# A transformer block in software pipeline on one core: outputs and feed-forward of a ahead of b, swaps and rotation in the turn of their projections

## The chip, the cores and the metric

The kernel runs on one core of a Trainium2 chip. Times are device microseconds of that core. A core has TensorE (PE in the profile, its weight loads as PEld), VectorE (DVE), ScalarE (ACT), GpSimd (POOL) and SyncE (SP), each with its own instruction queue that it works through in order; they wait for one another on semaphores. Here SP issues all DMAs.

## The reference, cut to what matters

Sixteen sequences of 512 tokens by 256 go through four residual steps, all in f32:

```python
x = x + attn_a(layernorm(x))   # 16 heads of 16, biases; window of |i-j| <= 32 and 4 global rows and columns; softmax
x = x + ffn(layernorm(x))      # int weights / 127; h = silu(gate) * up, 768 wide
x = x + attn_b(layernorm(x))   # num = exp(rotated q . k / 4), causal; den = sum(exp(unrotated q . k / 4)) over ALL keys
x = x + ffn(layernorm(x))      # the same weights
```

Attention b forms two sets of scores: of plain queries and keys for the denominator (512 keys, no mask), and of rotated ones for the numerator (causal).

## The kernel before, in words

**Slots.** Work is cut by sequence and pipelined in *slots*. In slot k each *block* of work handles sequence k minus its lag (`LAG`, a negative lag is a sequence ahead). The blocks: PA, VA, A are projections to queries and keys, values, and attention of a; OA its output projection and residual; F1 the first feed-forward; PB, VB, B, OB the same for attention b; RB the rotation; F2 the second feed-forward; NA the first layer norm of the next sequence. There are 20 slots, -1 to 18; slots 3 to 14 are a hardware loop of 12 turns, the others are written out. `ORDER` is the order in which the dense blocks take the two shared PSUM banks `gu_bank`; their counts (`GU`) turn it into semaphore values.

**The order of the work** is a table. `AT` gives each step a place on a line of about 125 units per slot; `places()` sorts them into `PLACES`, and every engine's function `slot()` walks that list and emits its part. So the same table sets the order on all five queues. The table's numbers are places, not times.

**Steps that the change touches.** Names are kinds in `PLACES`, lines those of the profile.
- *Projection* (T, PE L1038): six matmuls into a `gu_bank`; T1 on ACT takes the high half (L1174 of a, L1181 of b), T2 on DVE the low half (L1442, L1446); for b DVE also multiplies by cos into `tmp` (L1449).
- *Swap* (W, PE L1046): two matmuls with a permutation bring odd and even dimensions across. W1 on DVE multiplies by sin into `turned`, which lies in x1 (L1457). W2 is POOL's addition to `tmp` (L1563), ACT's high half (L1189), POOL's low half (L1565). The third and fourth DVE multiplication wait for POOL's first and second addition, as there are two `turned` buffers; the third and fourth swap wait for the first and second multiplication.
- *Packs* (UL plain, RL rotated, SL of a; SP L519): six DMAs bring a group of heads into the layout of the scores. For b there are four groups, two tiles each.
- *D* (PE L899, ACT L1137): 32 pairs of denominator scores and their exponentials. *N* (PE L920 and the mask L927, ACT L1127): 20 pairs of causal scores. Score banks are a ring of two pairs for A, D and N together. *BV* (PE L942): products with the values, *DT* the denominators' transpose, *BR* their reciprocals on DVE (L1321), for whose bank a later N pair waits.
- *X* (PE L985): transposes of a normalised sequence in `xn` into both `gu_bank`; X on ACT (L1155) and X1 on DVE (L1397) take the halves. *V* (PE L962): values, taken by DVE (L1471, L1473).
- *Outputs* (OL, SP L611, L593 for the reciprocals OR): the unprojected attention comes back from DRAM, both of a and of b into `on`, which is the memory of `xn`; DVE multiplies by the reciprocals (OM, L1340), splits into `h` (OH L1344, OW L1348), PE projects (O, L975), DVE adds to the residual (OX, L1357).
- *Maxima* (A1; PE L766, L774; DVE L1296): the first pass over the scores of a.
- *Feed-forward*: gate and up (G, U, PE L1010), tanh on ACT (L1166), DVE L1404, L1410, L1422, POOL L1558, down (D of F1 and F2, PE L1026), addition (E, L1436).
- XS stores a finished sequence, XA loads a new one into the same x2, XB and XL load x2 and x1.

## Time and profile before

| | us |
|---|---|
| median of 3 runs | 2675.46 (2670.17 to 2694.05) |
| profiled execution | 2662.93 |
| its span | 2661.1 |
| mean granted TensorE clock | 0.882 |
| loop of 12 slots | 371.7 to 2232.3 |

The columns of an engine are the time in which it works on something. "Idle before" in a timeline is how long the engine stood ahead of that instruction, and behind the arrow is what released it. PEclk is the share of full clock that TensorE was granted; it has two levels, 0.5 (1.2 GHz) and 1 (2.4 GHz), and a number between is a mix of stretches.

### The profile page before, as it was taken

The numbers are of one execution on the slowest core, as the hardware profiler recorded it, in microseconds if no ns is written. First come the engines' busy times: TensorE is split into PE (matmuls) and PEld (weight loads), VectorE is DVE, ScalarE is ACT, GpSimd is POOL, SyncE is SP. The second block draws the span as 40 slices with busy tenths as digits, with TensorE's granted clock in tenths as the row PEclk, the third lists the DMA queues.
The fourth block names the chain that finished last, engine by engine and source line by source line (L and its number), as shares of the span: only waits on it lengthen the run. The fifth ranks groups of instructions, "written<-read, shape, count | busy, mean of one in ns | idle before, by whom it ended". The sixth has DMA issues, their size and how long they took to land.

```text
span 2661.1 us, 73355 instructions
## 1 busy us (share of the span) xinstructions
PE 2178.7 (82%) x27269; PEld 1470.4 (55%) x27269; DVE 1359.7 (51%) x2972; ACT 1457.4 (55%) x3580; POOL 587.8 (22%) x619
## 2 busy tenths in 40 slices
PE   2567879888897988879798898979889798978785
PEld 2355446556564655646565565646656565645444
DVE  3355456463554656355464645556464555645433
ACT  1214655556465655646555574655557465656572
POOL 0013021221222222122221222222122223122311
PEclk7578889989898998989898898989899898988886
DMA  4223334241422415143241514224151423323221
GB/s 141 52 64 73 69 89 76 70 99 44 111 58 83 84 60 108 44 103 67 83 83 54 108 50 107 63 84 82 59 109 45 109 65 91 74 70 73 57 56 36
DMA packets 130030, 203.13 MB, mean 76 GB/s; under 512 B 27057, under 2 KB 60849, under 8 KB 129601
## 3 DMA queue, kind: packets, MB, share of 16 engines
q1 hardware_dynamic: 129632, 197.86, 31.0%
q8 instruction: 246, 4.03, 0.6%
q14 instruction: 152, 1.24, 0.2%
HBM read 67.93 MB, written 51.52 MB: 45 GB/s over the span
## 4 chain that ended last, share of the span: by engine, by line
issue 48%; PE 19%; POOL 13%; DVE 8%; ACT 5%; DMA 4%; SPq 2%; POOLq 0%; ACTq 0%; DVEq 0%
POOL h L1558 7%; PE gu_bank L1038 3%; PE gu_bank L1010 3%; ACT s_bank L1137 3%; DMA xn<-o_scr_B 2%; POOL x L1553 2%; PE d_bank L1026 2%; SPq L519 2%; PE gu_bank L985 1%; POOL root L1545 1%; PE o_bank L942 1%; POOL tmp L1563 1%; DVE top L1296 1%; PE gu_bank L975 1%; PE s_bank L899 1%
## 5 line engine op out<-in xcount | busy, mean ns | idle before, releaser
L1137 ACT ACTIVATE s_bank<-s_bank 128x512 f32<-128x512 f32 x1024 | 604.2, 591 | 167.0 <-PE s_bank L899 165.2
L1127 ACT ACTIVATE probs_B<-s_bank 128x512 f32<-128x512 f32 x640 | 345.4, 598 | 351.3 <-PE s_bank L927 346.7
L1558 POOL TENSOR_TENSOR h<-tmp,h 128x512 fp32r<-128x512 f32 x192 | 245.4, 1278 | 859.2 <-DVE h L1422 859.2
L1404 DVE SCALAR_TENSOR_TENSOR tmp<-tmp,gu_bank 128x512 f32<-128x512 f32 x192 | 131.6, 685 | 387.0 <-ACT tmp L1166 387.0
L899 PE MATMUL s_bank<-pack_b 48*128 48x512 f16 x1024 | 204.8, 411 | 84.9 <-ACT s_bank L1137 50.2
L1010 PE MATMUL gu_bank<-xT,w_g 128*128 128x256 f32 x1536 | 240.0, 295 | 18.4 <-DVE tmp L1404 15.5
L1026 PE MATMUL d_bank<-w_d,h 128*128 128x256 f32 x1536 | 235.9, 297 | 4.7 <-POOL h L1558 4.4
L1010 PE MATMUL gu_bank<-xT,w_u 128*128 128x256 f32 x1536 | 236.6, 293 | 0.4 <-DVE tmp L1410 0.4
L1010 PEld LDWEIGHTS gu_bank<-xT,w_g 128*128 128x128 f32 x1536 | 199.6, 191 | 46.7 <-DVE tmp L1404 21.6
L1026 PEld LDWEIGHTS d_bank<-w_d,h 128*128 128x128 f32 x1536 | 199.6, 193 | 34.7 <-issue 25.4
L1010 PEld LDWEIGHTS gu_bank<-xT,w_u 128*128 128x128 f32 x1536 | 197.3, 189 | 28.2 <-issue 15.8
L942 PE MATMUL o_bank<-probs_B,v_aug_B 128*16 128x512 f32 (+3 forms) x2048 | 183.5, 460 | 21.3 <-issue 20.3
L1137 ACT ACTIVATION_READ_ACCUMULATOR s_bank<-s_bank 128x1 f32 x1024 | 196.7, 192 | 0.0
L920 PE MATMUL s_bank<-pack_b 48*128 48x512 f16 (+3 forms) x1024 | 142.9, 340 | 45.0 <-DMA pack_b<-src_b 26.4
L1296 DVE TENSOR_REDUCE top<-s_bank 128x4 f32<-128x512 f32 x256 | 162.3, 683 | 19.3 <-PE s_bank L774 19.2
L1038 PE MATMUL gu_bank<-xT,wa_qk 128*128 128x512 f32 x384 | 140.5, 517 | 31.2 <-DVE xT L1397 16.7
L1117 ACT ACTIVATE probs_A<-s_bank 128x512 f32<-128x512 f32 x256 | 138.5, 595 | 48.6 <-PE s_bank L774 48.1
L985 PE MATMUL gu_bank<-eye,xn 128*128 128x128 f32 x512 | 99.3, 357 | 78.0 <-DVE x L1457 48.1
L899 PEld LDWEIGHTS s_bank<-pack_b 48*128 48x128 f16 x1024 | 48.2, 94 | 199.6 <-ACT s_bank L1137 81.4
L766 PE MATMUL s_bank<-band,eye_bf 64*64 64x512 bf16 x1024 | 110.6, 419 | 48.3 <-ACT s_bank L1137 16.2
L1166 ACT ACTIVATE tmp<-gu_bank 128x512 f32<-128x512 f32 x192 | 114.3, 595 | 62.8 <-PE gu_bank L1010 61.9
L1543 POOL TENSOR_TENSOR veps<-mv,eps 128x4 f32<-128x4 f32 x64 | 17.9, 280 | 571.0 <-DVE mv L1376 556.2
(145 smaller groups left out, 3409.0 us busy)
## 6 DMA issues: line engine op xcount, KB each, us to landing
pack_b<-src_b SPq DMA_DIRECT2D x768, 64.0 KB, 2.3
pack_a<-src_a SPq DMA_DIRECT2D x384, 64.0 KB, 2.3
x<-in_L_attn_a_x_dram SPq DMA_DIRECT2D x32, 512.0 KB, 4.1
o_scr_A<-o_raw SPq DMA_DIRECT2D x64, 256.0 KB, 2.0
o_scr_B<-o_raw SPq DMA_DIRECT2D x64, 256.0 KB, 2.2
rden_on<-r_scr_A SPq DMA_DIRECT2D x32, 256.0 KB
xn<-o_scr_A SPq DMA_DIRECT2D x32, 256.0 KB
x_scr<-x SPq DMA_DIRECT2D x16, 512.0 KB, 3.0
```

What stands on the lines that cost most here:

```text
L899: pe.matmul(score_bank(s, "D", q, e)[:, :], pack_b[r, j % 2, 0, 0, tile, t * P:(t + 1) * P], pack_b[r, j % 2, 0, 1, tile, :], start=True, ...
L920: pe.matmul(bank[e][:, c0:c0 + S - t * P], pack_b[r, j % 2, 1, 1, tile, t * P:(t + 1) * P], pack_b[r, j % 2, 1, 0, tile, t * P:S], start=i ...
L942: last = pe.matmul(o_bank[32 * c:32 * c + DH, t * P:S], v_aug["B"][:, t, head(j, c), 0:DH], probs["B"][:, (j * NU_B + n) % RING, c0:c0 + S ...
L1010: last = pe.matmul(gu_bank[up][:, f * D:(f + 1) * D], plain(w[:, k, c:c + P], exact), plain(given[:, k, half * D:(half + 1) * D], exact), ...
L1026: last = pe.matmul(bank[:, t, :], plain(h[part][:, i % 2, c:c + P], exact), plain(w_d[:, 2 * pair + f, :], exact), start=pair == 0 and f = ...
L1038: last = pe.matmul(bank[:, :], w_part[:, k, n * P:(n + 1) * P], given[part][:, k, :], start=k == 0 and i == 0, stop=k == KT - 1 and i == 2)
L1117: act.activation(dst, given, ACT.Exp, scale=SM_SCALE).then_inc(a_exp, 1)
L1127: act.activation(probs["B"][:, n % RING, :], score_bank(s, "N", n // 2, n % 2)[:, :], ACT.Exp, scale=SM_SCALE)\
L1137: act.activation(bank[:, :], bank[:, :], ACT.Exp, scale=SM_SCALE, accum_out=den[:, 0, j, 2 * tile + e, t:t + 1]).then_inc(den_exp, 1)
L1296: dve.reduce_max(dst, a, AX.X).then_inc(a1_taken, 1)
L1404: dve.scalar_tensor_tensor(t, t, 1.0, gu_bank[0][:, :], ALU.add, ALU.mult).then_inc(gu_taken, 1)
L1558: pool.tensor_tensor(h[1][:, i % 2, :], tmp[:, i % 2, :], h[0][:, i % 2, :].bitcast(F32), ALU.subtract)\
```

## The change

`ORDER` and `LAG` change and with them the whole table `AT`; places of every kind differ.
- OA and F1 stand ahead of OB and F2 in the order of the dense blocks. Before it was OB, OA, F2, F1.
- RB has lag 1 instead of 2 and stands behind PB: swaps and rotation run in the slot in which their projections ran, at its end, and no longer at the start of the next one.
- The first two of the four plain and of the four rotated packs (UL, RL with n below 2) move with them, from the slot of the scores to the end of the one before.
- Outputs of b get a tile of their own, `on_b`, and the semaphore `on_in` becomes one for each block. Loading them no longer waits for the transposes that empty `xn`; loading those of a does, and stands first in SP's slot.
- `d_at`, `rot_taken` and some waits follow the new order. The places of pairs within a group may alternate in distance (`DQ`, `NQ`).

```diff
@@ -56,9 +56,9 @@
-LAG = {"A": 0, "B": 2, "VB": 2, "RB": 2, "PA": 0, "VA": 0, "OB": 3, "OA": 1, "F2": 3, "F1": 1, "PB": 1, "NA": -1}
-ORDER = ("VB", "RB", "PA", "VA", "OB", "OA", "F2", "F1", "PB", "NA")
-LNS, FS, OS, PS = ("F2", "F1", "PB", "NA"), ("F2", "F1"), ("OB", "OA"), ("PA", "PB")
+LAG = {"A": 0, "B": 2, "VB": 2, "PA": 0, "OA": 1, "VA": 0, "OB": 3, "F1": 1, "F2": 3, "PB": 1, "RB": 1, "NA": -1}
+ORDER = ("VB", "PA", "OA", "VA", "OB", "F1", "F2", "PB", "RB", "NA")
+LNS, FS, OS, PS = ("F1", "F2", "PB", "NA"), ("F1", "F2"), ("OA", "OB"), ("PA", "PB")
 GU = {"VB": 2, "RB": 4, "PA": 6, "VA": 2, "OB": 2, "OA": 2, "F2": 2 + 2 * FT, "F1": 2 + 2 * FT, "PB": 6}
 DU = {"F2": 2, "F1": 2}
 FIRST, STEADY = 3, 12
@@ AT
...
-    "UL": (1.19, 5.67, 40.11, 57.67), "RL": (20.82, 24.52, 44.53, 71.33),
...
-    "VB": (2.46, 2.46), "VBC": (2.46, 2.46), "VA": (23.96, 23.98), "VAC": (18.96, 24.59), "GW": 23.5, "GL": 32.18,
-    "W": (3.02, 3.05, 4.83, 8.68), "W1": (4.63, 6.29, 8.66, 8.94), "W2": (0.47, 3.71, 9.62, 11.19),
...
-    "OB": (10.43, 13.39, 16, 16.06, 17.65, 18.76, 24.01, 24.54, 26.33, 29.05),
-    "OA": (26.61, 27.57, 29.44, 29.9, 30.81, 31.98, 32.2, 33.86, 32.4, 34.47),
...
+    "DQ": (0, 0, 0, 0.16), "NQ": (0.9, 0.13, 0.74, 0),
...
+    "UL": (114.15, 120.36, 33.05, 49.37), "RL": (123.52, 124, 34.9, 64.9),
...
+    "VB": (0, 0), "VBC": (0, 0), "VA": (22.6, 24.48), "VAC": (22.9, 25.71), "GW": 25.48, "GL": 30.38,
+    "W": (109.15, 110.6, 111.15, 114.13), "W1": (110.95, 115.4, 122.82, 124), "W2": (111.11, 121.14, 121.42, 122.37),
...
+    "OA": (6.62, 9.02, 10.36, 11.2, 11.58, 16.52, 18.35, 19.2, 19.37, 21.69),
+    "OB": (22.27, 22.61, 22.88, 24.01, 24.18, 25.34, 25.57, 26.88, 27.95, 30.37),
...
@@ -117,15 +118,16 @@
     for j in range(GROUPS):
         for q in range(8):
-            put(AT["D"][j] + AT["DS"][j] * q, "D", 8 * j + q, "B")
+            put(AT["D"][j] + AT["DS"][j] * (q - AT["DQ"][j] * (q % 2)), "D", 8 * j + q, "B")
         for p in range(5):
-            put(AT["N"][j] + AT["NS"][j] * p, "N", 5 * j + p, "B")
+            put(AT["N"][j] + AT["NS"][j] * (p - AT["NQ"][j] * (p % 2)), "N", 5 * j + p, "B")
     for kind in ("BV", "BT", "BO"):
         for n, place in enumerate(AT[kind]):
             put(place, kind, n, "OB" if n == len(AT[kind]) - 1 else "B")
     for kind in ("DT", "BR", "BW"):
         put(AT[kind], kind, 0, "B")
-    puts("UL", "UL", "B"), puts("RL", "RL", "B")
+    for n in range(GROUPS):
+        put(AT["UL"][n], "UL", n, "B" if n >= 2 else "PB"), put(AT["RL"][n], "RL", n, "B" if n >= 2 else "RB")
     for block in ("VB", "VA"):
@@ -341,7 +343,8 @@
         den_a = sb("den_a", [HEADS * NT, P], F32)
         rden = {b: sb(f"rden_{b}", [HEADS * NT, P], F32) for b in "AB"}
         o_raw = [sb(f"o_raw{i}", [P, S], F32) for i in range(2)]
-        on = xn[:, :, :].rearrange("p t n -> p (t n)").rearrange("p (u s) -> p u s", u=KT)
+        on_b = sb("on_b", [P, KT, S], F32)
+        ON_OF = {"OA": xn[:, :, :].rearrange("p t n -> p (t n)").rearrange("p (u s) -> p u s", u=KT), "OB": on_b}
         rden_on = sb("rden_on", [P, KT, S], F32)
         tmp = sb("tmp", [P, 4, S], F32)
         h = [sb(f"h{i}", [P, 2, S], F32R) for i in range(2)]
@@ -400,7 +403,7 @@
         rden_ready = {b: sem(f"rden_ready_{b}") for b in "AB"}
         rden_out = {b: sem(f"rden_out_{b}") for b in "AB"}
         rden_in = sem("rden_in")
-        on_in = sem("on_in")
+        on_in = {b: sem(f"on_in_{b}") for b in "AB"}
         on_scaled = sem("on_scaled")
         on_high = sem("on_high")
         on_ready = sem("on_ready")
@@ -448,7 +451,7 @@
         st_f32 = [stage(st_a, 0, FT * D), stage(st_a, FT * D, FT * D), stage(st_probs, 0, FT * D)]
         st_ocols = stage(st_a, 2 * FT * D, KT, D)
         st_dT = stage(st_probs, FT * D, FT, D)
-        st_o = on[:, 0, :].rearrange("p (t n) -> p t n", t=KT)
+        st_o = on_b[:, 0, :].rearrange("p (t n) -> p t n", t=KT)
         st2 = src_b[:, :, :, :, :, :].rearrange("p a b c d s -> p (a b c d s)").bitcast(F32)
         st_gT = st2[:, 0:KT * HID].rearrange("p (k n) -> p k n", k=KT)
         st_uT = st2[:, KT * HID:2 * KT * HID].rearrange("p (k n) -> p k n", k=KT)
@@ -532,7 +535,7 @@
                 if j == 0 and rotated:
                     sp.wait_ge(rot_ready, ((seq + 1) * 4).at(turn))
                 elif j == 0:
-                    sp.wait_ge(gu_taken, (s.last().gu("PB") + 6).at(turn))
+                    sp.wait_ge(gu_taken, (s.gu("PB") + 6).at(turn))
                 if j >= 2:
                     sp.wait_ge(scores, (seq * units + units // GROUPS * (j - 1)).at(turn))
                 elif seq.some:
@@ -573,7 +576,7 @@
                 sp.wait_ge(o_taken, (take + 1).at(turn))
                 if earlier_o is not None:
-                    sp.wait_ge(on_in, ((earlier_o + 1) * 32).at(turn))
+                    sp.wait_ge(on_in[kind], ((earlier_o + 1) * 32).at(turn))
                 sp.dma_start(o_scr[kind][j], o_raw[at][:, :]).then_inc(o_out[at], 16)
             def store_reciprocals(s, kind, turn):
@@ -601,14 +604,15 @@
             def load_outputs(s, o, turn):
                 kind = o[1]
-                if s.nth(OS, o).some:
-                    sp.wait_ge(on_ready, (s.nth(OS, o) * KT).at(turn))
-                sp.wait_ge(xT_high, (s.nth(LNS, o) * KT).at(turn))
-                if kind == "B":
+                if kind == "A":
+                    sp.wait_ge(xT_high, (s.nth(LNS, o) * KT).at(turn))
+                else:
+                    if s.seq[o].some:
+                        sp.wait_ge(on_ready, (s.nth(OS, OS[0]) * KT).at(turn))
                     all_stored(s, "B", turn)
                 for u in range(KT):
                     rows = o_scr[kind].rearrange("(u j) (c r) s -> u (j c) r s", u=2, c=4)[u, :, 0:DH]
-                    sp.dma_start(on[:, u, :], rows).then_inc(on_in, 16)
+                    sp.dma_start(ON_OF[o][:, u, :], rows).then_inc(on_in[kind], 16)
             def load_denominators(s, turn):
                 seq = s.seq["A"]
@@ -626,7 +630,7 @@
                         load_maxima(s, turn)
                     elif kind in ("AO", "BO") and block in "AB":
                         o = "O" + block
-                        store_output(block, n, *s.take(block, n), s.staged(block, n), s.nth(OS, o) if s.here[o] else None, turn)
+                        store_output(block, n, *s.take(block, n), s.staged(block, n), s.seq[o] if s.here[o] else None, turn)
                     elif kind == "BO":
                         store_output("B", n, *s.take("B", n), s.staged("B", n), None, turn)
                     elif kind == "AD":
@@ -653,7 +657,7 @@
                         if s.here["F2"]:
                             sp.wait_ge(x_stored, ((s.seq["F2"] + 1) * 16).at(turn))
                         elif s.seq["NA"].some:
-                            sp.wait_ge(xn_ready, (s.nth(LNS, "VB") * NT).at(turn))
+                            sp.wait_ge(xn_ready, (s.nth(LNS, ORDER[0]) * NT).at(turn))
                         sp.dma_start(x2[:, :, :], x_in[bass.ds(s.seq["NA"].at(turn), 1)].rearrange("a (t p) n -> p (a t) n", p=P))\
                             .then_inc(x2_new, 16)
                     elif kind == "XB":
@@ -667,8 +671,8 @@
                         sp.wait_ge(x1_done, (s.seq["PB"] + 1).at(turn))
                         sp.dma_start(x_scr[bass.ds(s.seq["PB"].at(turn), 1)].rearrange("a p t n -> p (a t) n"), x1[:, :, :]).then_inc(x1_out, 16)
                     elif kind == "XL":
-                        if s.here["RB"]:
-                            sp.wait_ge(rot_sum, ((s.seq["RB"] + 1) * 4).at(turn))
+                        if s.last().here["RB"]:
+                            sp.wait_ge(rot_sum, ((s.last().seq["RB"] + 1) * 4).at(turn))
                         sp.dma_start(x1[:, :, :], x_in[bass.ds(s.seq["OA"].at(turn), 1)].rearrange("a (t p) n -> p (a t) n", p=P))\
                             .then_inc(x1_in, 16)
@@ -1041,7 +1045,7 @@
             def swap_step(s, n, turn):
                 bank = gu(s, "RB", n, turn)
-                pe.wait_ge(*rot_taken(s.last(), n, turn))
+                pe.wait_ge(*rot_taken(s, n, turn))
                 for i in range(2):
                     last = pe.matmul(bank[:, :], swap[:, :], src_b[:, 0, n // 2, i, n % 2, :], start=i == 0, stop=i == 1)
                 last.then_inc(gu_ready, 1)
@@ -1336,16 +1340,17 @@
             def o_scaled(s, block, u, turn):
                 if u == 0:
                     dve.wait_ge(rden_in, ((s.nth(OS, block) + 1) * 32).at(turn))
-                    dve.wait_ge(on_in, ((s.nth(OS, block) + 1) * 32).at(turn))
+                    dve.wait_ge(on_in[block[1]], ((s.seq[block] + 1) * 32).at(turn))
+                on = ON_OF[block]
                 dve.tensor_tensor(on[:, u, :], on[:, u, :], rden_on[:, u, :], ALU.mult).then_inc(on_scaled, 1)
             def o_high(s, block, u, turn):
                 dve.wait_ge(on_scaled, (s.nth(OS, block) * KT + (u + 1)).at(turn))
-                dve.tensor_copy(h[0][:, u, :], on[:, u, :]).then_inc(on_high, 1)
+                dve.tensor_copy(h[0][:, u, :], ON_OF[block][:, u, :]).then_inc(on_high, 1)
             def o_low(s, block, u, turn):
                 dve.wait_ge(on_high, (s.nth(OS, block) * KT + (u + 1)).at(turn))
-                dve.tensor_tensor(h[1][:, u, :], on[:, u, :], h[0][:, u, :].bitcast(F32), ALU.subtract).then_inc(on_ready, 1)
+                dve.tensor_tensor(h[1][:, u, :], ON_OF[block][:, u, :], h[0][:, u, :].bitcast(F32), ALU.subtract).then_inc(on_ready, 1)
             def o_added(s, block, half, turn):
                 xs = X_OF[block][:, 2 * half:2 * half + 2, :]
@@ -1423,12 +1428,7 @@
             def d_at(s, block, earlier_one):
-                if not earlier_one:
-                    return s.d(block)
-                if block == "F1" and s.here["F2"]:
-                    return s.d("F2")
-                last = s.last()
-                return last.d("F1" if last.here["F1"] else "F2")
+                return s.d(block) + -2 if earlier_one else s.d(block)
             def ffn_added(s, block, half, turn):
                 xs = X_OF[block][:, 2 * half:2 * half + 2, :]
```

What moves, first on PE at the turn of the loop. L1046 is a swap, L983 and L985 the transposes of PA, L899 a D pair. Before, in the middle of a slot's first steps:

```order
L953 ISA
L1044 ISA
L1046 MATMUL gu_bank<-src_b,swap 128x512 x2
L953 ISA
L1044 ISA
L1046 MATMUL gu_bank<-src_b,swap 128x512 x2
L953 ISA
L1044 ISA
L1046 MATMUL gu_bank<-src_b,swap 128x512 x2
L953 ISA x2
L983 ISA
L985 MATMUL gu_bank<-eye,xn 128x128 x2
```

After, at the end of the loop's body (all lines are 4 higher there: L1050 a swap, L924 and L931 an N pair, L946 values):

```order
L943 ISA
L946 MATMUL o_bank<-probs_B,v_aug_B 16x512 x4
L742 REGISTER_ALU
L924 MATMUL s_bank<-pack_b 128x384 x2
L924 MATMUL s_bank<-pack_b 128x128 x2
L931 MATMUL s_bank<-causal,eye_bf 64x128 x8
L744 ISA
L924 MATMUL s_bank<-pack_b 128x256 x4
L931 MATMUL s_bank<-causal,eye_bf 64x128 x8
L957 ISA
L1048 ISA
L1050 MATMUL gu_bank<-src_b,swap 128x512 x2
```

and at the start of the body (L903 the first D pair, L966 the V step, L989 the transposes of PA):

```order
L744 ISA
L903 MATMUL s_bank<-pack_b 128x512 x2
L957 ISA
L966 MATMUL gu_bank<-wb_v,xT 128x256 x12
L957 ISA
L966 MATMUL gu_bank<-wb_v,xT 128x256 x12
L943 ISA
L946 MATMUL o_bank<-probs_B,v_aug_B 16x256 x4
L957 ISA x2
L987 ISA
L989 MATMUL gu_bank<-eye,xn 128x128 x2
```

The four swaps stood one behind the other with the transposes next. Now pairs and value batches stand between the swaps, and D0 and the V step between the last one and the transposes.

Second, on SP. Before, in the first third of the slot, where L519 is the second plain pack and L611 the load of the outputs of b:

```order
L539 ISA
L519 DMA pack_b<-src_b 16x2x1024 [waits den_scores]
L519 DMA pack_b<-src_b 16x2x1024
L519 DMA pack_b<-src_b 16x2048 x2
L519 DMA pack_b<-src_b 16x2x1024 x2
L605 ISA
L606 ISA [waits on_ready]
L600 ISA [waits xT_high]
L600 ISA [waits o_out1]
L611 DMA xn<-o_scr_B 128x1x512 [waits o_out0]
L611 DMA xn<-o_scr_B 128x1x512
```

After, at the end of the body (L522 a pack, first the second plain one; L669 is XB, the L522 behind it rotated packs):

```order
L522 DMA pack_b<-src_b 16x2x1024 x2
L665 ISA
L668 ISA [waits xn_ready]
L669 ISA [waits x1_out]
L669 DMA x<-x_scr 128x1024
L536 ISA
L542 ISA [waits rot_ready]
L522 DMA pack_b<-src_b 16x2x1024 [waits b_scores]
L522 DMA pack_b<-src_b 16x2x1024
L522 DMA pack_b<-src_b 16x2048 x2
L522 DMA pack_b<-src_b 16x2x1024 x2
L542 ISA
```

and behind the turn (L615 the load of the outputs of a, L596 the reciprocals, L676 is XL):

```order
L681 ISA
L615 DMA xn<-o_scr_A 128x1x512 [waits xT_high]
L615 DMA xn<-o_scr_A 128x1x512
L591 ISA
L593 ISA [waits rden_out_A]
L596 DMA rden_on<-r_scr_A 128x1x512 [waits on_scaled]
L596 DMA rden_on<-r_scr_A 128x1x512
L577 ISA
L580 DMA o_scr_B<-o_raw 128x512 [waits o_taken]
L675 ISA
L676 ISA [waits rot_sum]
L676 DMA x<-in_L_attn_a_x_dram 128x4x256
```

The load that opens the slot's outputs stood behind two plain packs and waits for the transposes; now it is that of a, and in SP's queue it stands behind both rotated packs, of which the first waits for `rot_ready`.

## Rows read from the trace of the kernel before

**Rows 1.** The page: span, and busy time, share, instructions of each engine.

```profile
span 2661.1 us, 73355 instructions
...
PE 2178.7 (82%) x27269; PEld 1470.4 (55%) x27269; DVE 1359.7 (51%) x2972; ACT 1457.4 (55%) x3580; POOL 587.8 (22%) x619
```

**Rows 2.** Windows: length, busy (instructions) of PE, PEld, DVE, ACT, POOL, PEclk, DMA.

```profile
371.70:2232.30 1860.60, 1601.51 (x20414) 1085.46 (x20412) 998.92 (x2208) 1087.32 (x2676) 438.42 (x456) 0.91 0.33 78
2512.10:2610.00 97.90, 69.90 (x571) 35.18 (x569) 30.08 (x58) 66.76 (x180) 18.62 (x16) 0.79 0.29 65
```

**Rows 3.** Windows within one slot, the same columns.

```profile
1470.00:1480.50 10.50, 8.73 (x24) 5.42 (x24) 2.11 (x4) 5.84 (x14) 6.12 (x6) 0.51 0.51 122
1496.00:1504.50 8.50, 6.29 (x64) 4.11 (x60) 4.72 (x16) 3.15 (x6) 1.57 (x2) 0.60 0.63 101
1504.50:1588.00 83.50, 79.87 (x1248) 56.50 (x1246) 45.54 (x92) 55.34 (x138) 16.81 (x15) 1.00 0.29 63
1588.00:1600.00 12.00, 8.28 (x74) 4.35 (x69) 7.52 (x29) 10.10 (x27) 2.89 (x5) 0.72 0.07 25
1490.31:1529.00 38.69, 32.71 (x409) 22.75 (x407) 29.66 (x72) 16.89 (x43) 6.97 (x9) 0.91 0.54 99
```

**Rows 4.** Waits of PE in the loop: who, for whom: us, times, longest.

```profile
PE gu_bank L985 <- DVE x L1457: 40.6, 12, 3.4
PE gu_bank L975 <- DVE h L1348: 24.8, 12, 2.3
...
PE s_bank L920 <- DMA pack_b<-src_b: 19.9, 12, 2.3
...
PE gu_bank L1046 <- DVE x L1457: 7.6, 14, 0.6
...
PE gu_bank L1046 <- DVE v_aug_B L1473: 4.7, 12, 0.5
```

**Rows 5.** Timeline of PE: start us, us, what, and in brackets idle before.

```profile
1459.15 0.62 PE L942 MATMUL o_bank<-probs_B,v_aug_B 128*16 128x256 f32 x8 [1.74 <-issue]
...
1464.17 0.61 PE L1046 MATMUL gu_bank<-src_b,swap 128*128 128x512 f16 x2
...
1471.04 1.96 PE L985 MATMUL gu_bank<-eye,xn 128*128 128x128 f32 x8 [3.38 <-DVE x L1457]
...
1474.28 2.92 PE L1038 MATMUL gu_bank<-xT,wa_qk 128*128 128x512 f32 x6 [0.74 <-DVE xT L1397]
...
1481.78 1.68 PE L1038 MATMUL gu_bank<-xT,wa_qk 128*128 128x512 f32 x6 [0.64 <-DVE src_a L1442]
...
1487.40 3.08 PE L962 MATMUL gu_bank<-wa_v,xT 128*128 128x256 f32 x24
...
1495.44 0.39 PE L920 MATMUL s_bank<-pack_b 48*128 48x512 f16 x2 [2.10 <-DMA pack_b<-src_b]
...
1498.72 1.65 PE L975 MATMUL gu_bank<-wa_o,h 128*128 128x256 f32 x6 [2.21 <-DVE h L1348]
```

**Rows 6.** Timeline of POOL, first and last of the eight rotation steps.

```profile
1465.80 1.26 POOL L1563 TENSOR_TENSOR tmp<-tmp,x 128x512 f32<-128x512 f32 x1 [17.03 <-DVE x L1457]
...
1478.52 1.16 POOL L1565 TENSOR_TENSOR src_b<-tmp,src_b 128x512 f16<-128x512 f32 x1 [1.61 <-ACT src_b L1189]
```

**Rows 7.** Timeline of SP: a pack's six DMAs, an output's two.

```profile
1467.79 3.82 SPq L519 DMA_DIRECT2D pack_b<-src_b  x6
1474.10 1.30 SPq L611 DMA_DIRECT2D xn<-o_scr_B  x2
```

**Rows 8.** Timeline of DVE: outputs of b, first multiplication and low halves.

```profile
1480.37 0.69 DVE L1340 TENSOR_TENSOR xn<-xn,rden_on 128x512 f32<-128x512 f32 x1 [5.63 <-DMA xn<-o_scr_B]
...
1485.30 1.28 DVE L1348 TENSOR_TENSOR h<-xn,h 128x512 fp32r<-128x512 f32 x2
```

**Rows 9.** Timeline of PE in the stretch of the maxima.

```profile
1518.68 0.39 PE L899 MATMUL s_bank<-pack_b 48*128 48x512 f16 x2 [1.04 <-DVE top L1296]
```

**Rows 10.** Timeline of PE in the slot from 2512, first causal pair.

```profile
2536.32 0.39 PE L920 MATMUL s_bank<-pack_b 48*128 48x512 f16 x2
```

2 lines of the change are left out of this document (1 added, 1 removed), and 32 rows, old and new, of the table AT.

## The prediction

> **What bounds the kernel now.** I read the page first, then the windows by slot, the waits of TensorE in the loop, and the timeline of one slot. The page [rows 1] has PE busy for 82% of the span and no other engine, its own weight loads included, above 55%. The loop, 12 of the 20 slots, runs from 371.7 to 2232.3 us: 1860.6 us, 155.05 us a slot, with PE busy for 1601.5 of them, 133.5 a slot, at a mean granted clock of 0.91 [rows 2]. So PE sets the pace, and there are only two things to win: the 21.6 us a slot in which it stands, and the work that it does at the lower of its two clock levels (1.2 instead of 2.4 GHz). Both lie together. The windows of one slot [rows 3] show a stretch of 83.5 us at clock 1.00 with PE busy for 79.9 of them: nothing is to be had there. At 1470 to 1480.5 the clock is 0.51, at 1496 to 1504.5 0.60, at 1588 to 1600 0.72, and each of these follows or holds standing time. The change is to be judged in these three places.
>
> **The change part by part**, in us per full slot, the turn of the loop being time S.
>
> *a. Swaps and rotation go from the start of the slot to the end of the one before.* Nothing is added or removed: four swaps, four DVE multiplies, eight POOL operations, four ACT copies. Before, the swaps stand in a row and the transposes of PA behind them need the fourth multiply, which waits for POOL. PE waits 40.6 + 7.6 + 4.7 = 52.9 us in 12 slots on these, 4.4 a slot [rows 4], the largest wait being 3.38 us ahead of the transposes [rows 5]. In the new order the third and fourth swap have causal pairs and value batches between them, then come the turn, D0 and the V step, so the POOL chain has cover. What stays is PA's transposes waiting for the V bank to be copied out; the copy is one DVE operation after the V step, and I put it at 0.7, the size of the nearest waits of that kind (0.74 and 0.64 [rows 5]). **-3.7**; bounds -4.4 and 0.
>
> *b. The rotated packs are loaded before the turn.* The first rotated pair waits for its pack now: 19.9 us in 12 slots, 1.7 each [rows 4]. Later it has the first half of the slot as cover, and if the loads end at S+14 it still comes at about S+22. **-1.7**. The plain packs move from the start of the slot to the end of the previous one as well. D0 becomes the first PE instruction; its load can be issued when PB's last projection is taken, costs SP 3.8 and lands some 2 us later, against about 11 us of pairs, swaps and value batches. No cost; without that cover it would be 6.
>
> *c. Outputs of a go first, and SP reaches their load later.* This is the cost of the change. SP executes in order, and the load of the outputs of a now stands behind both rotated packs, which wait for the last POOL operation of the rotation. By hand: between the first swap and the turn PE has four swaps (0.61 each), four causal pairs (0.39 for the two products of one, plus their masks), value batches (the smallest 0.62, the others put at 1), and the turn itself, 1.74 [rows 5]: 9 us, so the first multiply lies about 8 us before S. The rotation takes from 1465.80 to 1479.68, 13.9 us [rows 6]: it ends at S+6. Two packs at 3.82 us of SP each [rows 7]: S+14. From the issue of such a load to the first multiplication of the outputs the trace has 1474.10 to 1480.37, 6.3 us [rows 7, 8]; from there to the end of the low half 1480.37 to 1486.58, 6.2, with other work between, and under 4 without it [rows 8]. h is ready at S+24 to S+26.5. PE: D0, V step, value batch and wait bring it to the transposes at about S+6.5; from the transposes to the output step it needed 1471.04 to 1490.31 [rows 3, 5], 19.3 us, holding a V step of 3.1 that comes later now, and one more D; two causal pairs come in, so 17 us: S+23.5. It stands 0.5 to 3; I take 2.5, near the upper end, because waits on the way to the V step push nothing forward. Today the same place costs 24.8 / 12 = 2.1 [rows 4]. **+0.4**; bounds -2.1 (no wait) and +3.9 (a wait of 6). The trace shows 6.3 us from issue to use [rows 7, 8]. The Trainium skill (DMA: Bandwidth & Descriptors, section "Anatomy of one DMA — SWDGE (gpsimd) path") gives about 2.0 us fixed plus the bytes at 436 GB/s, for another issuing path; 2.6 us for 256 KB. By it the wait would be gone and this term -2.1; the measured interval decides here.
>
> *Outputs of b in a tile of their own* removes the wait for xn; their load is behind nothing on PE for 10 us more. Its wait on PE before was small (the 24.8 is mostly a's, at 2.21 in the slot shown [rows 5]). 0.
>
> *d. The end of the slot.* Now PE stands 12.0 - 8.28 = 3.7 of 12 us at 1588 to 1600 [rows 3], on ACT: the last D pairs and first causal pairs come faster than exponentials. PB's four projections, today bunched at the very end, stand among these pairs in the new order. Against that, the eighth causal pair waits for the reciprocal of b, which DVE now has behind a layer norm and a multiply. **-1.2**; bounds -3.7 and +2.
>
> *e. Clock.* In the stretch at 0.51 a projection of six matmuls took 2.92 us, at full clock 1.68 [rows 5]: two of these alone lose 2.5, with the transposes and pairs of the stretch I put 4. Without the 3.4 us of standing before them it need not fall. But a shorter wait and the turn remain, and at 1496 a wait of two times 2.1 also ends at 0.60 [rows 3]. **-2**; bounds 0 and -4. The Trainium skill (TensorE: Matmul & The Clock Gate, section "HAM oscillation — how this bites in real kernels") says that recurring waits put the array back to its low level each time; by it the whole stretch recovers once the wait goes, and the sum has 2 us more gain per slot. The trace agrees as far as every low stretch has a wait at its start.
>
> *f. Density on DVE.* From the output step of b on, DVE is busy 29.66 of 38.69 us [rows 3]. In the new order both output blocks, both layer norms, the values of a and the maxima of a stand closer together, the maxima ending ten places earlier. PE waits 1.04 us for a maximum there once [rows 9]; one or two more of these: **+1.5**; bounds 0 and +8.
>
> Sum: -3.7 - 1.7 + 0.4 - 1.2 - 2 + 1.5 = **-6.7 us a slot**. It holds in the 12 slots of the loop and the one after, 13: -87. The slot at 2512 has only b's attention beside outputs and feed-forward; the swaps and rotation at its head delay its pairs, the first causal one comes at 2536.32, 24 us in [rows 2, 10]. Without them -8. First slots with b: +1 (D0 waits there for its pack, as no pairs cover it). The slot before the last two: -2. Together -96. The profiled execution took 2662.93 us (span 2661.1): 2567. The runs' median, 2675.46, is 12.5 above it; the same 96 from there give 2579.5, and I forecast **2580**.
>
> **The rivals.**
> *R1, nothing moves but the name of the wait (17%).* The transposes no longer wait, but V, D0 or the eighth causal pair does, for the same chain DVE, POOL, ACT. For it: in the new order ACT has the last three rotation copies in a row, ahead of D0's exponential. Against: 11 us of PE work between. Terms a and e fall out: -1.0 a slot, -22 in all: 2653.
> *R2, DVE becomes the bound in the stretch of the maxima (13%).* If each of the eight pairs of maxima makes PE wait as the one in [rows 9], f is 8 and not 1.5: -0.2 a slot, with the ends -12: 2664. For it: 77% busy there already. Against: in 83.5 us at full clock, PE is never held by it for long.
> *R3, slower: SP reaches the outputs of a too late (10%).* Term c with a later rotation. If ACT's rotation copies are held behind the last exponentials, or SP behind the reciprocals of a, the whole queue slides, and every us beyond S+14 is one for PE at the output step, and its clock falls (e is lost, +2). At S+25 it is +11 + 2 - 6.7 = +6.3 a slot, 13 times, less 9: 2748. It decides for slower than now from a load issued at about S+19, by over 1% from S+21.
>
> **How the numbers follow.** My forecast has 60%; its own range, terms within half their bounds, is 2535 to 2630. The range for 8 in 10 takes in R1 and R2 and nearly all of the case with c, d and e at their better ends (-12 a slot, 2510): 2520 to 2680. Within 1% of 2675.46, 2648.7 to 2702.2, is what a measurement can't tell from no change. Faster: 60% and 8 of R1's 17 and 2 of R2's: 70%. Same: 9 + 10 = 19%. Slower: R3 and a little of R2: 11%.
>
> **What would show it.** Right: no wait above 1 us ahead of the transposes of PA; no wait of the first causal pair for a DMA; the clock at 1.00 in the first 20 us of a slot; loop slots of 147 to 150 us; the wait for h before the output step of a at 1 to 4 us. Wrong: a wait of over 6 us there, with the load of xn issued after S+18 (R3); PE waits for maxima over 5 us a slot (R2); PE idle before the V step or the last causal pairs (R1); or PE busy time per slot that does not fall although its waits do.

## The result: slower by 2.5%, where 3.6% faster was forecast

| | before | after |
|---|---|---|
| median | 2676.29 us (4 runs beside it) | 2742.92 us (4 runs, 2739.84 to 2745.40) |
| ratio, 95% interval | | 1.025, 1.0195 to 1.0305 |
| span of the profiled execution | 2661.1 us | 2738.0 us |
| a slot of the loop | 155.05 us | 160.55 us |
| PE busy in it | 133.5 us | 133.4 us |

A second measurement on another chip gave 2746.14 us, ratio 1.0286 (1.0224 to 1.0348). The forecast was 2580 with a range of 2520 to 2680. The sign was wrong too; the case that ended slower, R3, had 10%. That its 2748 lies near the measured time is chance: it came from a load issued at S+25, and the load went out at S+15.

The page of the changed kernel, which answers to [rows 1]:

```profile
span 2738.0 us, 73312 instructions
...
PE 2168.2 (79%) x27269; PEld 1482.0 (54%) x27269; DVE 1426.1 (52%) x2972; ACT 1450.5 (53%) x3580; POOL 603.2 (22%) x619
```

And windows, with the columns of [rows 2]: the loop of 12 slots, and the end of the program behind it.

```profile
363.10:2289.66 1926.56, 1600.78 (x20424) 1097.99 (x20417) 1060.35 (x2210) 1083.09 (x2677) 451.54 (x457) 0.91 0.32 76
2289.66:2738.00 448.34, 334.39 (x3275) 222.61 (x3271) 195.31 (x406) 234.56 (x604) 95.55 (x91) 0.84 0.27 64
```

The loop went from 1860.6 to 1926.6 us, 66.0 more, with the same PE busy time and the same clock. So these 5.5 us a slot are time in which PE stands. The program before the loop is 8.6 us shorter (371.7 to 363.1), the end behind it 19.5 longer (2661.1 - 2232.3 = 428.8 to 448.3): 66.0 - 8.6 + 19.5 = 76.9, the difference of the spans. In the end, too, it is the wait for `h`, 16.1 us at 4 output steps before and 47.1 at 6 now.

Waits of PE in the loop of the changed kernel: who, for whom, us in total, times, longest. They answer to [rows 4]. L979 is the output projection, L989 the transposes, L1042 a projection, L1050 a swap, L924 a causal pair, L903 a D pair.

```profile
PE gu_bank L979 <- DVE h L1353: 82.5, 24, 6.2
PE s_bank L924 <- ACT s_bank L1141: 33.9, 36, 1.4
PE s_bank L903 <- issue: 31.0, 11, 3.1
PE s_bank L770 <- DVE top L1300: 21.4, 35, 0.9
PE gu_bank L989 <- DVE v_aug_B L1473: 20.6, 12, 1.7
PE s_bank L903 <- ACT s_bank L1141: 19.2, 39, 1.2
PE s_bank L903 <- DVE top L1300: 18.4, 20, 1.2
PE gu_bank L1042 <- DVE xT L1402: 16.7, 12, 1.5
...
PE gu_bank L1050 <- DVE x L1457: 8.7, 22, 0.5
```

The largest is new in size and in number: 82.5 us, 6.9 a slot, ahead of 24 output steps, both of each slot, where 12 steps with 24.8 us waited before. The rows of the swaps and of the first causal pair's pack, 52.9 and 19.9 us before, are 29.3 and none.

One slot shows how the wait comes about. It is the one with the longest wait for the outputs of a, 6.24 us; over the 12 slots these waits run from 1.6 to 6.2 and are 3.8 in the mean. Its turn is S = 1646.69. PE:

```profile
1646.69 0.39 PE L903 MATMUL s_bank<-pack_b 48*128 48x512 f16 x2 [2.65 <-issue]
...
1653.90 1.09 PE L989 MATMUL gu_bank<-eye,xn 128*128 128x128 f32 x8 [1.72 <-DVE v_aug_B L1473]
1656.37 1.66 PE L1042 MATMUL gu_bank<-xT,wa_qk 128*128 128x512 f32 x6 [1.38 <-DVE xT L1402]
...
1667.75 0.39 PE L924 MATMUL s_bank<-pack_b 48*128 48x512 f16 x2 [1.39 <-ACT s_bank L1141]
...
1676.05 5.49 PE L979 MATMUL gu_bank<-wa_o,h 128*128 128x256 f32 x24 [6.24 <-DVE h L1353]
...
1691.47 2.26 PE L979 MATMUL gu_bank<-wb_o,h 128*128 128x256 f32 x12 [2.47 <-DVE h L1353]
```

SP's queue in the same slot:

```profile
1653.73 7.79 SPq L522 DMA_DIRECT2D pack_b<-src_b  x12
1662.06 1.31 SPq L615 DMA_DIRECT2D xn<-o_scr_A  x2
1663.58 1.19 SPq L596 DMA_DIRECT2D rden_on<-r_scr_A  x2
...
1665.57 0.40 SPq L676 DMA_DIRECT2D x<-in_L_attn_a_x_dram  x1
1674.22 1.24 SPq L596 DMA_DIRECT2D rden_on<-r_scr_B  x2
1675.66 1.19 SPq L615 DMA_DIRECT2D on_b<-o_scr_B  x2
1677.06 16.45 SPq L522 DMA_DIRECT2D pack_a<-src_a  x24
```

And DVE:

```profile
1672.90 1.29 DVE L1345 TENSOR_TENSOR xn<-xn,rden_on 128x512 f32<-128x512 f32 x2 [5.63 <-DMA rden_on<-r_scr_A]
1674.11 0.75 DVE L1349 CAST h<-xn 128x512 fp32r<-128x512 f32 x2
1674.78 2.35 DVE L1353 TENSOR_TENSOR h<-xn,h 128x512 fp32r<-128x512 f32 x2
...
1684.88 0.69 DVE L1345 TENSOR_TENSOR on_b<-on_b,rden_on 128x512 f32<-128x512 f32 x1 [2.62 <-DMA on_b<-o_scr_B]
```

Read together: twelve DMAs of two rotated packs hold SP from S+7.0 to S+14.8. The outputs of a are issued behind them at S+15.4 and their reciprocals at S+16.9; DVE uses both at S+26.2, `h` is there at S+30.4 (its first half a little earlier), and PE, done with its pairs at S+23.1, stands 6.24 us. The output step then runs at a granted clock of 0.50: 24 matmuls in 5.49 us. In the median of the slots the first multiplication is at S+24.5 and the output step at S+27.6. For b, the reciprocals share the tile `rden_on` with those of a, so SP issues their load at 1674.22, right behind DVE's second multiplication of a, and the outputs of b behind that; DVE has them 9.2 us later, and PE stands 2.47 us. SP's waits in the loop have this as a row of its own, 6.9 us a slot:

```profile
SPq L596 <- DVE xn L1345: 82.9, 12, 8.1
```

### The profile page after: what moved, and what is told of

It is laid out like the page before. It is cut to its first block, busy times and chain, and to the rows that moved or that the text cites. A ratio compares the mean times of both kernels' runs of the same rounds, so it can differ in the third digit from the quotient of the medians.

```text
span 2738.0 us, 73312 instructions
## 1 busy us (share of the span) xinstructions
PE 2168.2 (79%) x27269; PEld 1482.0 (54%) x27269; DVE 1426.1 (52%) x2972; ACT 1450.5 (53%) x3580; POOL 603.2 (22%) x619
## 4 chain that ended last, share of the span: by engine, by line
issue 50%; PE 18%; POOL 14%; DVE 6%; ACT 6%; DMA 3%; SPq 3%; POOLq 0%; DVEq 0%; ACTq 0%
POOL h L1558 7%; PE gu_bank L1042 3%; ACT s_bank L1141 3%; POOL x L1553 3%; PE gu_bank L1014 3%; POOL root L1545 2%; PE gu_bank L966 2%; SPq L522 2%; PE o_bank L946 2%; PE d_bank L1030 1%; DMA rden_on<-r_scr_A 1%; PE s_bank L903 1%; PE gu_bank L979 1%; DMA on_b<-o_scr_B 1%; PE gu_bank L989 1%
## 5 line engine op out<-in xcount | busy, mean ns | idle before, releaser
L1131 ACT ACTIVATE probs_B<-s_bank 128x512 f32<-128x512 f32 x640 | 336.6, 600 | 306.3 <-PE s_bank L931 305.6
L903 PE MATMUL s_bank<-pack_b 48*128 48x512 f16 x1024 | 207.0, 410 | 119.3 <-ACT s_bank L1141 46.2
L1030 PE MATMUL d_bank<-w_d,h 128*128 128x256 f32 x1536 | 229.2, 292 | 10.3 <-POOL h L1558 9.5
L1014 PEld LDWEIGHTS gu_bank<-xT,w_g 128*128 128x128 f32 x1536 | 205.1, 196 | 45.6 <-issue 22.3
L1014 PEld LDWEIGHTS gu_bank<-xT,w_u 128*128 128x128 f32 x1536 | 207.4, 197 | 23.4 <-issue 13.7
L946 PE MATMUL o_bank<-probs_B,v_aug_B 128*16 128x512 f32 (+3 forms) x2048 | 188.4, 465 | 0.9 <-ACT probs_B L1131 0.6
L903 PEld LDWEIGHTS s_bank<-pack_b 48*128 48x128 f16 x1024 | 48.1, 94 | 236.7 <-ACT s_bank L1141 85.0
L924 PE MATMUL s_bank<-pack_b 48*128 48x512 f16 (+3 forms) x1024 | 133.5, 320 | 53.8 <-ACT s_bank L1141 44.4
L770 PE MATMUL s_bank<-band,eye_bf 64*64 64x512 bf16 x1024 | 112.8, 428 | 57.3 <-DVE top L1300 25.5
L1402 DVE TENSOR_TENSOR xT<-gu_bank,xT 128x512 fp32r<-128x512 f32 x128 | 82.4, 686 | 134.0 <-ACT xT L1159 133.0
L1042 PE MATMUL gu_bank<-xT,wa_qk 128*128 128x512 f32 x384 | 122.5, 463 | 26.1 <-DVE xT L1402 24.5
```

Source lines behind the costliest of these rows:

```text
L903: pe.matmul(score_bank(s, "D", q, e)[:, :], pack_b[r, j % 2, 0, 0, tile, t * P:(t + 1) * P], pack_b[r, j % 2, 0, 1, tile, :], start=True, ...
L924: pe.matmul(bank[e][:, c0:c0 + S - t * P], pack_b[r, j % 2, 1, 1, tile, t * P:(t + 1) * P], pack_b[r, j % 2, 1, 0, tile, t * P:S], start=i ...
L946: last = pe.matmul(o_bank[32 * c:32 * c + DH, t * P:S], v_aug["B"][:, t, head(j, c), 0:DH], probs["B"][:, (j * NU_B + n) % RING, c0:c0 + S ...
L1014: last = pe.matmul(gu_bank[up][:, f * D:(f + 1) * D], plain(w[:, k, c:c + P], exact), plain(given[:, k, half * D:(half + 1) * D], exact), ...
L1030: last = pe.matmul(bank[:, t, :], plain(h[part][:, i % 2, c:c + P], exact), plain(w_d[:, 2 * pair + f, :], exact), start=pair == 0 and f = ...
L1042: last = pe.matmul(bank[:, :], w_part[:, k, n * P:(n + 1) * P], given[part][:, k, :], start=k == 0 and i == 0, stop=k == KT - 1 and i == 2)
```

## Experiments

Two theories were set against each other throughout. **Q**: SP's queue (what stands ahead of a load, and which tile it waits for) sets the output steps, and this is what the change costs. **Renamed**: PE meets some other limit in the first 30 us of a slot, or the denser work on DVE, so that taking one wait away only moves it. Each result gives the ratio to the kernel before on the same chip, with its 95% interval. Per-slot numbers are those of 12 slots of the loop in the profile; the windows begin at another point of the slot than those above, hence 160.3 for the changed kernel here and 160.55 there. The ratios are not those of the medians to the last digit, and where it matters the text gives both. Two measurements of one kernel lie up to 0.5% and two of its profiles up to 1.3 us a slot apart (r2_tile and r5_tile).

| run | edit | median us | ratio (interval) | us a slot | PE waits for h, first / second output block |
|---|---|---|---|---|---|
| before | | 2662.5 to 2672.6 | 1 | 154.9 | 0.0 / 2.1 |
| r1_after | none, the change | 2746.14 | 1.0286 (1.0224, 1.0348) | 160.9 | 4.9 / 3.1 |
| r1_rl1 | second rotated pack later | 2680.42 | 1.0038 (0.9985, 1.0091) | 157.3 | 1.5 / 2.6 |
| r1_rl01 | both rotated packs later | 2661.34 | 0.9969 (0.9921, 1.0016) | 155.7 | 1.2 / 1.8 |
| r1_va | values of a earlier | 2748.18 | 1.0299 (1.0247, 1.0350) | 160.9 | 4.0 / 6.3 |
| r2_tile | before + own tile | 2632.51 | 0.9874 (0.9796, 0.9952) | 152.6 | 0.0 / 2.4 |
| r2_rot | before + rotation moved | 2744.75 | 1.0269 (1.0191, 1.0347) | 162.1 | 0.0 / 1.7 |
| r2_rl01_va | both packs later + values earlier | 2722.69 | 1.0192 (1.0119, 1.0265) | 161.1 | 2.6 / 6.6 |
| r2_all | the same + reciprocals of a earlier, value batch ahead of the V step | 2710.82 | 1.0155 (1.0081, 1.0229) | 159.5 | 2.7 / 6.5 |
| r3_three | both packs later + reciprocals of a earlier, value batch first in the slot | 2666.37 | 0.9987 (0.9959, 1.0015) | 156.2 | 1.8 / 1.8 |
| r3_order | before + own tile + dense order | 2658.03 | 0.9947 (0.9920, 0.9974) | 153.9 | 0.0 / 2.4 |
| r3_xl | load of x later | 2804.07 | 1.0491 (1.0457, 1.0525) | 165.7 | 3.3 / 0.1 |
| r3_pool | three additions of POOL left out | 2734.07 | 1.0227 (1.0193, 1.0261) | 160.0 | 4.0 / 3.3 |
| r4_rot | before + own tile + rotation moved, load early | 2693.37 | 1.0083 (1.0052, 1.0114) | 159.2 | 0.0 / 2.1 |
| r4_packs | before + own tile + packs ahead of outputs of a | 2758.68 | 1.0308 (1.0263, 1.0353) | 162.4 | 0.0 / 9.7 |
| r4_early | both packs later, own tile to a | 2672.65 | 0.9988 (0.9960, 1.0015) | 156.3 | 0.0 / 0.95 |
| r4_mult | before + own tile, multiplication early | 2638.28 | 0.9862 (0.9809, 0.9915) | 153.9 | 0.0 / 2.6 |
| r5_recip | no load of reciprocals of b | 2665.77 | 0.9990 (0.9959, 1.0020) | 156.6 | 4.3 / 0.0 |
| r5_tile | before + own tile, again | 2652.05 | 0.9929 (0.9895, 0.9963) | 153.9 | 0.0 / 2.5 |

Edits are to the changed kernel unless the table says "before". The first block is that of a in the changed kernel and in r3_order, and that of b in the kernel before and its other versions.

### The packs ahead of the outputs: r1_rl1, r1_rl01, r1_va

```diff
# r1_rl1
-    ... "RL": (123.52, 124, 34.9, 64.9),
+    ... "RL": (123.52, 8.9, 34.9, 64.9),
# r1_rl01
+    ... "RL": (5.6, 8.9, 34.9, 64.9),
# both: a pack placed here belongs to block "B" of this slot, not to "RB" of the slot before
```

> The second rotated pack is issued behind both output loads instead of ahead of them. Theory Q (SP's queue sets the output step of a): the loads of the outputs of a and its reciprocals are issued 3.8 us earlier and share the DMA engines with six transfers fewer; the wait for h falls from 6.9 to 2 to 3 us a slot, the time by 3.5 to 5 us a slot, 50 to 75 us in all: 2670 to 2695. Theory D (density: the causal pairs behind ACT and the maxima behind DVE made the slot long, PE would meet these waits anyway): the wait moves to others, the time falls by less than 15 us: over 2725.

> Both rotated packs are issued behind the loads of the outputs of a (the first behind x1's load, the second behind the outputs of b). Theory Q: the output loads come when PA is transposed (8 us earlier than now is not possible, since they wait for that), the wait for h is nearly gone, but the first causal pair may wait again for its pack, 0 to 2 us a slot: 2655 to 2690. Theory D: over 2725.

One pack moved behind the outputs of b gives 3.6 us a slot back, both give 5.2, and the time is that of the kernel before. Both times lie in Q's ranges; in r1_rl1 4.1 us a slot of waits for `h` are left where 2 to 3 were expected. PE waits in the loop with both packs later:

```profile
PE gu_bank L979 <- DVE h L1353: 35.9, 22, 2.7
PE s_bank L903 <- issue: 30.5, 11, 3.1
PE s_bank L924 <- DMA pack_b<-src_b: 25.5, 8, 4.1
```

The wait for `h` falls to 35.9 us, from 82.5 above and 96.5 in r1_after on the same chip, and that of the first causal pair for its pack is back (25.5, before 19.9). PE busy falls as well, from 132.9 to 131.3 us a slot, at a mean granted clock of 0.93 instead of 0.92. Taking the packs from ahead of the outputs is worth 84.8 us, and the change is 80.5 slower than the kernel before on that chip. It moves SP's issues and takes transfers from beside the loads at once; these runs do not part the two.

r1_va is the rival's test. It gives DVE and PE the values of a ahead of the outputs of a.

```diff
-ORDER = ("VB", "PA", "OA", "VA", "OB", ...
+ORDER = ("VB", "PA", "VA", "OA", "OB", ...
-    "VA": (22.6, 24.48), "VAC": (22.9, 25.71),
+    "VA": (9.5, 12.3), "VAC": (6.55, 6.6),
```

> SP's queue is left; the V step of a (3.1 us of PE at full clock) goes ahead of the causal pairs and the output step of a. Theory Q: PE uses 3.1 us of its 6.2 us wait, the clock falls later, the wait for h is about 3.5 to 4 us a slot: 2690 to 2710. Theory D in its ACT part: the waits of the first two causal pairs behind exponentials (2.0 us in the slot looked at) vanish as well, the wait for h stays: 2710 to 2720.

2748.18, nothing, where both expectations had a gain: 3 us of PE work put ahead of the step take 0.9 us off the first block's wait (4.9 to 4.0), and the second block's, which this work stood in front of before, grows from 3.1 to 6.3. An output step that is set by a transfer is not helped by work moved in front of it. With the packs later (r2_rl01_va), the same edit costs 61 us.

### The parts one by one on the kernel before: r2_tile, r5_tile, r3_order, r2_rot

```diff
# r2_tile: the tile on_b and a semaphore on_in for each block; outputs of b wait for on_ready, no longer for xT_high
# r3_order: r2_tile, and
-ORDER = ("VB", "RB", "PA", "VA", "OB", "OA", "F2", "F1", "PB", "NA")
+ORDER = ("VB", "RB", "PA", "VA", "OA", "OB", "F1", "F2", "PB", "NA")
# with the places of OA/OB, F1/F2 exchanged, XS, XA at 105.05, 105.1, and the first two of NAN later
# r2_rot: RB with lag 1 behind PB, and
-    "W": (3.02, 3.05, 4.83, 8.68), "W1": (4.63, 6.29, 8.66, 8.94), "W2": (0.47, 3.71, 9.62, 11.19),
+    "W": (123.5, 123.6, 123.7, 123.9), "W1": (123.55, 123.6, 123.7, 123.9), "W2": (123.6, 123.7, 123.8, 124),
```

> The kernel before with one part of the change alone: the outputs of b in a tile of their own (order of blocks, lags and table as before). Theory Q: the load of the outputs of a, which in this order comes second, still waits for the transposes only and not for the outputs of b to be split, but SP stands in the same order, so the change is under 0.7 us a slot: 2655 to 2675. Theory T (the separate tile is what costs, by more DMA traffic at once): over 2690.

2632.51, below its range: the tile, costed at nothing, is worth 30 us, or 16 to 19 (by medians, by ratio) by the second measurement. It is the one part that is faster beyond its interval both times. SP's queue shows why. Waits of SP in the loop, first the kernel before, then the own tile:

```profile
SPq L606 <- DVE h L1348: 31.7, 11, 3.6
...
SPq L600 <- ACT xT L1155: 16.9, 11, 2.8
```

```profile
SPq L594 <- DVE on_b L1343: 33.0, 11, 4.3
```

Before, SP stood for the casts of the outputs of b before it could load those of a into the same memory, and behind it stood the two rotated packs. With the own tile this wait is gone (that for the shared reciprocals stays), the first rotated pack goes out 23.9 us after the turn instead of 28.9, and PE's wait for a pack falls from 1.66 to under 0.5 us a slot.

> The kernel before with the own tile for outputs of b alone, measured again in more rounds. Where the tile brings 2.3 us a slot, as one profile had it: ratio 0.983 to 0.990, and its interval lies below that of the new order alone (0.992 to 0.997). Rival (the first measurement was a lucky one, and tile and order together are worth the same as the tile): 0.991 to 0.997.

0.9929, in the rival's range: the first measurement was on the lucky side, and the interval overlaps that of tile and order together (0.9920 to 0.9974). Both intervals lie below 1, so the own tile is worth 0.7 to 1.3%.

> The kernel before with the own tile for outputs of b and with the dense blocks in the new order alone: outputs of a take the places of those of b and the other way round, the two feed-forwards likewise, the store of a finished sequence and the load of the new one come behind the second of them; swaps, rotation and all packs stay where they were. Compare the own tile alone: 2632.5 us. Theory Q: no load is put behind another in SP's queue, so the order of blocks itself costs and brings nothing on PE in the loop; 2625 to 2650, and the ends of the program a little different. Rival D (the new order is what costs, since outputs, both layer norms and maxima stand closer on DVE, and the layer norm of the new sequence comes behind the second feed-forward's end): +3 a slot or more, 2665 to 2690, seen as waits for maxima, for x or for xn.

2658.03. It lies between the two cases, and its interval meets both of the tile's. The new order of the dense blocks is worth 0 to +1.3 us a slot; no wait of PE in its profile grows by more than 0.7. It is not what costs 66 us.

> The kernel before with another part alone: swaps and rotation directly behind their projections, ahead of the turn, all packs and outputs as before. If this move is good by itself, PE's 3.4 us wait ahead of the transposes of PA goes, while ACT and PE at the turn have no other work to put between (0 to 1.5 us new): 2625 to 2660. If the move only renames the wait (the chain DVE, POOL, ACT held by the rest): 2660 to 2700.

2744.75, a clear miss: the rotation's move alone costs 82 us (72 by the ratio) where the expectation had 2 to 37 to gain and its rival at most 37 to lose. PE's waits in the loop:

```profile
PE gu_bank L1038 <- DVE src_a L1442: 49.2, 12, 6.0
PE o_bank L942 <- issue: 33.6, 11, 3.5
...
PE gu_bank L1038 <- DVE xT L1397: 29.0, 12, 3.4
```

The 3.4 us ahead of the transposes are gone, and 4.1 stand at the projections of PA. DVE comes there early now, at the multiplication of the outputs of b, which its table puts ahead of PA's low halves, and stands 7.8 us for a transfer that is not there yet. The rotation had covered it.

### Is it the load, or the move itself? r4_rot, r4_packs

```diff
# r4_rot: r2_tile and r2_rot together, and
-    "OL": (10.6, 17.47), ...  "OB": (10.43, 13.39, 16, ...
+    "OL": (3.0, 17.47), ...   "OB": (13.39, 13.4, 16, ...
# r4_packs: r2_tile, and
-    "RL": (20.82, 24.52, 44.53, 71.33),
+    "RL": (15, 15.5, 44.53, 71.33),
```

> The kernel before with the own tile for outputs of b and with swaps and rotation at the end of the slot, as in the run that did this alone (2744.8 us), but with the load of outputs of b at place 3.0 instead of 10.6 and its two multiplications at 13.4, behind the first low half of PA instead of ahead of it. In that run DVE stood 7.8 us at the multiplication with the low halves of PA queued behind it, and PE 5.5 us for src_a. Theory Q (the cost of the rotation's move is only this load and its place in DVE's queue): the wait for src_a is gone, that of the transposes is 0.9 instead of 3.4: 150.5 to 152.5 us a slot, 2610 to 2635 us. Rival (the move itself costs, four swaps in a row at the end of the slot with POOL's chain bare, 1.5 more at the turn and PE's clock low): 2665 to 2710.

2693.37: some of both. The wait for `src_a` fell from 4.1 to 1.8 us a slot, and of the 82 us 61 went (50 of 72 by the ratios; 19 to 30 of them by the tile). But it stays 41 to 61 us above the own tile alone, and the rival's causes are there: the turn 2.8 us (33.5 in 12 slots) instead of 1.9, swaps that wait 17.8 us for `tmp`, PE busy 134.8 instead of 132.2 us a slot. My places bunch the four swaps more than the change's do, so this run bounds the move from above only.

> The kernel before with the own tile for outputs of b (2632.5 us), and the two rotated packs at places 15 and 15.5 instead of 20.8 and 24.5, which puts them ahead of the loads of the reciprocals and outputs of a. That is the changed kernel's sequence on SP in the old order of blocks. They wait for the rotation's end, 20 us after S, and take SP 8 us; outputs of a are then issued at S+29 and not S+22.5. Theory Q: the wait for h of a grows by 3 to 5 us a slot, the small wait of the first causal pair for its pack goes (-0.4), 2670 to 2695 us. Rival (packs ahead of outputs do no harm, since the outputs of a have cover in the old order): 2625 to 2640.

2758.68, ratio 1.0308, slower than Q had it. Two numbers in the table, and the fastest version of the old order loses 3.8 to 4.4%. The loop's largest wait:

```profile
PE gu_bank L977 <- DVE h L1351: 116.6, 12, 10.9
```

It was 28.7 with the own tile alone. SP issues the outputs of a at 1380.54 there, DVE's multiplication starts at 1389.33, after standing for them:

```profile
1389.33 1.29 DVE L1343 TENSOR_TENSOR xn<-xn,rden_on 128x512 f32<-128x512 f32 x2 [6.61 <-DMA xn<-o_scr_A]
```

8.8 us from issue to use, with 24 packs of a issued right behind, where I had reckoned with 6.3; that is 2.5 of the 2.3 to 4.3 us by which the wait exceeds the expectation. Here, too, packs ahead of the outputs of a make PE wait, in a kernel that shares neither the changed order of blocks nor its rotation.

### The second block: r5_recip

```diff
             def load_reciprocals(s, o, turn):
                 kind = o[1]
+                if kind == "B":
+                    return
```

It multiplies the outputs of b by the reciprocals of a, so it leaves out this part of the computation.

> The changed kernel without the load of the reciprocals of b (outputs of b are multiplied by those of a, so this part of the computation is wrong in it). In the changed kernel that load is issued only when DVE has multiplied the outputs of a, since both use one tile, and the load of the outputs of b is behind it in SP's queue, issued 1.4 us later and used 9.2 us after that. Theory Q (queue and shared tile hold b): outputs of b are loaded right behind x, some 9 us earlier, the wait for h of b falls from 3.0 to under 0.7 us a slot, the wait for h of a stays at 3.8 to 5; 2700 to 2722 us. Rival 1 (b's turn on DVE, behind the addition of a and the layer norm, is what holds it): its wait stays above 2, 2732 to 2750. Rival 2 (three transfers together slow those of a): the wait for h of a grows by what b wins, 2732 to 2755.

2665.77: 34 us better than Q's best case. The wait of b for `h` went from 3.0 to none:

```profile
PE gu_bank L981 <- DVE h L1356: 52.0, 12, 6.5
```

Twelve waits are left of 24, all of a. The loop is 3.8 us a slot shorter: 3.0 by this wait and 1.5 by PE's busy time (133.2 to 131.7), less 0.5 by which a's wait grew. The ratio to before is 0.999, as with both packs later. So either of two repairs undoes the whole loss. No run has both, but they can't be added in full: with both packs later and hardly a wait for `h` left (r4_early) the time is the same again.

The road was not the expected one, though. The outputs of b go out at S+25.2 (median), 2.2 us earlier than the 27.4 of the changed kernel and not 9, because SP now stands for the store of b's last outputs to DRAM, 6.7 us a slot:

```profile
SPq L605 <- DMA o_scr_B<-o_raw: 80.3, 13, 7.6
```

And they are multiplied 8 us behind their issue, without DVE standing for them, where it was 9.3. So of the 3.4 us by which this multiplication comes earlier, 2.2 are SP's: its issuing of the reciprocals, 1.5 us, and what is left of the wait for the shared tile, since SP would otherwise have stood for the store through most of it. The rest comes with the reciprocals' own transfer gone.

### What else was tried

```diff
# r3_xl
-    "XL": 5.47, ...
+    "XL": 8.85, ...
# r3_pool: of POOL's four additions of the bias to x of a, one is left
-                for t in range(NT):
+                for t in range(1 if block == "OA" else NT):
```

> The changed kernel with one number changed: the load of x for the output step of a (512 KB) at place 8.85 instead of 5.47, that is behind the loads of the reciprocals and of the outputs of b and not right behind those of a. Theory Q with sharing (the 9.3 us from the issue of the load of the reciprocals to the first multiplication, against 6.3 before, are there because 512 KB are on their way beside them): the wait for h before the outputs falls from 8.0 by 2 to 3 us a slot, 2705 to 2725 us. Rival: the 9.3 us are there because 12 packs were issued just ahead, and nothing changes: 2735 to 2755. Second rival: x comes too late for the bias and addition of the outputs of a, DVE stands for it, and it is slower: 2755 to 2790.

2804.07, the second rival and worse than it. POOL had no x to add the bias to, DVE stood for POOL at the addition of a, so the bank came free late, and PE stood 8.5 us a slot ahead of the values of a (101.9 in 12 slots). The sharing that it was to show is small: the outputs of a are used 8.8 us after their issue instead of 9.5.

> The changed kernel without three of POOL's four additions of the bias to x of a (it leaves this part of the computation out). They run beside DVE's low halves of the outputs of a, of which the first took 2.35 us there and 1.28 us where POOL did nothing. Theory of shared access (DVE and POOL slow each other when both work in SBUF): the low halves fall to 1.3 to 1.5 us, the wait for h by 1 us a slot, 2725 to 2740 us. Rival (the longer time has another cause, such as the transfers that land): L1353 stays above 2 us and the time at 2740 to 2752.

2734.07, ratio 1.0227 against 1.025 and 1.0286. The low half fell from 1081 to 866 ns in the mean, the wait for `h` did not (7.3 us a slot against 6.9 and 8.0). The time is in the theory's range, but the two low halves together take 1.7 us and not 1.3 to 1.5. DVE is slower beside POOL here, and it is not the cause.

> The changed kernel with both rotated packs behind the outputs of a, and with the V step of a ahead of the first causal pairs. Theory Q: alone the V step did nothing since the output step was held by SP's loads; with SP freed it fills what is left there: of 2.1 us for the pack and 3.0 for h, 2 to 3.5 a slot go: 2615 to 2640. If the output step is held by something else now (DVE's rows between), under 10 us of difference to the 2661 of the packs alone.

> The same, and the reciprocals of a loaded ahead of the outputs of a (SP stands there idle, waiting for the transposes), and the last value batch of b ahead of the V step, since DVE's copy of the values waits for it and PA's transposes wait 1.7 us a slot for that copy. Theory Q: another 1 to 2 us a slot: 2595 to 2625.

```diff
# r2_rl01_va: r1_rl01 and r1_va together; r2_all: also
-    "OR": (2, 6.76), ... "BV": (..., 0.21), ... "VB": (0, 0), "VBC": (0, 0)
+    "OR": (0.5, 6.76), ... "BV": (..., 0.05), ... "VB": (0.1, 0.12), "VBC": (0.15, 0.17)
# r3_three: r1_rl01, and of r2_all all but the values of a; D0 behind the value batch
```

Both missed, by 83 and 86 us. The values of a ahead of the outputs of a put the second block's loads later (its reciprocals wait for a's multiplication on DVE), and its wait is 6.5 us a slot in both: the reciprocals of b are issued at S+25.4 in r2_rl01_va and at S+22.3 in r1_rl01.

> The changed kernel with three things put right at once: all four rotated packs are loaded in the slot of their scores (places 5.6 and 8.9, behind the outputs of a), the reciprocals of a are loaded at place 0.5, ahead of the plain pack and of the outputs of a, and the turn begins with the last value batch of b, so that DVE can copy the values of b at once. It differs from the run with the rotated packs alone (2661.3 us, 155.65 us a slot) in the last two. Theory Q (what SP and DVE do in their turn sets the output step and the transposes): the wait of the transposes of PA for v_aug_B falls from 1.70 to 0.9 us a slot, the wait for h from 3.0 to 2, the standing at the turn from 2.54 to the 1.7 that the kernel before has with a value batch in this place: -2.6 a slot, 2625 to 2640 us. Rival (the waits are only renamed): PE is held by ACT's exponentials there anyhow, whose waits were 6 us a slot: 2652 to 2668. It would then not beat the kernel before with a tile of its own for the outputs of b (2632.5).

The rival's: 2666.37. The wait for `v_aug_B` fell from 1.70 to 0.92 us a slot as expected, and the standing at the turn stayed at 2.5, so the value batch in this place is not what made it 1.7 before. ACT's waits took the gain.

```diff
# r4_early: r1_rl01, and the two tiles exchanged (ON_OF), with
-    "OL": (0.91, 8.79), "OR": (2, 6.76), "OA": (6.62, 9.02, 10.36, 11.2, 11.58, 16.52, ...
+    "OL": (0.3, 8.79), "OR": (0.2, 6.76), "OA": (1.3, 5.2, 6.56, 6.57, 6.6, 6.7, ...
# r4_mult: r2_tile, and "OL": (3.0, 17.47), "OA": (24.6, 24.7, ...
```

> The changed kernel with all rotated packs behind the outputs of b in the slot of their scores (2661.3 us in a run of that alone) and with the two tiles exchanged: outputs of a get the tile of their own and are loaded at place 0.3, those of b share memory with xn. So the load of a waits neither for PA's transposes nor for packs, and its multiplications stand between the low halves of PA. Theory Q: the wait for h of a goes, 3.0 to 1 us a slot for both blocks, 2632 to 2645 us. Rival (waits are renamed: with h early PE only meets ACT's exponentials and copies of PA sooner, as in the run with three things put right): 2655 to 2672.

The rival's again: 2672.65. The wait for `h` is 0.95 us a slot in all, none of it ahead of the outputs of a. In its place stand:

```profile
PE s_bank L924 <- ACT s_bank L1141: 29.1, 27, 2.6
PE gu_bank L1042 <- DVE src_a L1442: 28.2, 10, 4.9
```

DVE now stands for the outputs of a ahead of PA's low halves, as in r2_rot.

> The kernel before with the own tile for outputs of b (2632.5 us), its load at place 3.0 instead of 10.6, and DVE's two multiplications of outputs of a ahead of the first addition of b instead of behind it. In the run with the own tile DVE waited 0.7 us for PE at that addition while reciprocals and outputs of a had long landed, and PE then waited 2.1 us for h of a. Theory Q: that wait falls from 2.4 by about 1.2 us a slot: 2612 to 2622 us. Rival (PE is held at the same place by ACT's exponentials or the pack of the first causal pair instead): 2628 to 2638.

2638.28, 0.9862, at the edge of the rival's range: no gain over the own tile. PE's wait did not fall (2.6 for 2.4), so the order of DVE's two multiplications was not its cause.

## Why the prediction was wrong

By its own steps, us a slot, from [rows 4] and the waits above:

| step | forecast | measured |
|---|---|---|
| a, swaps and rotation | -3.7 | -2.0, and most of it taken back at the turn and the transposes |
| b, rotated packs early | -1.7 | -1.7 |
| c, outputs of a | +0.4 | **+1.7** (3.8 against 2.1) |
| c, outputs of b | 0 | **+3.0** |
| d, end of slot | -1.2 | -1.9 in its last 30 us; ACT's waits over the whole slot +3.0 (4.6 to 7.6) |
| e, clock | -2 | 0 (PE busy 133.5 to 133.4) |
| f, density on DVE | +1.5 | +1.9 |

The rows of waits (a, b, c, ACT's of d, f) sum to +5.9, the turn adds 0.9, and the other waits take about 1.3 off: +5.5.

Two things went wrong. Step c explains why the change is slower than before: with either half of it repaired the time is even. The way from even to -96 us is the gains of a, d and e: with c repaired they did not come either.

**Step c failed, in its second sentence most.** I costed the outputs of b at nothing because "their load is behind nothing on PE for 10 us more". PE was the wrong queue to look in. SP's queue has the reciprocals of b ahead of them, and these wait for DVE to be done with the reciprocals of a in the same tile (the row of 82.9 us above); r5_recip takes this one load away, and the 3.0 are gone, the loss with them. It shows this load to be the cause, by 2.2 us in SP's queue and the rest where its transfer is gone. How much the tile alone would give, with the load kept, was not run. The prediction also took the 24.8 us of before to be mostly a's; they are a's altogether.

**Its first half had the timetable right and the transfer wrong.** Packs done at S+14 (S+14.8 in the slot shown), PE at the step at S+23.5 (23.1). But between issue and use I took 6.3 us [rows 7, 8] from a load whose reciprocals had been there for long. Here outputs, reciprocals and x are issued within 4 us, and the first use is 10.8 us after the first of them (9.5 in the median). DVE's last wait is that for the reciprocals, which go out 1.5 us behind the outputs: that is about half of the 3.2 us by which the median exceeds 6.3. With 6.3 from S+15.4 the wait would have been near the forecast. R3 had this mechanism and was read too mildly: it let the load slip to S+19 before it decides, and with the real transfer it decides at S+15. Of its own signs, a wait of over 6 us showed in one slot of 12, and "issued after S+18" did not; by its mean of 3.8 this wait even lies within the 1 to 4 us that the prediction named as a sign of being right.

r1_rl1 and r1_rl01 show the step to be the cause: one and two packs moved in SP's order, and 3.6 and 5.2 us a slot. r4_packs shows it without the rest of the change.

**Step e hung on c, and on more than c.** PE busy did not fall, and the prediction had named that as a sign. Where the wait is taken away it falls by 1.2 to 1.9 us a slot (r5_recip, r1_rl01, against the two profiles of the changed kernel), near the 2 forecast. Two profiles of one kernel differ by up to 0.8 here (r2_tile, r5_tile), so this is a rough figure. The granted clock of the output steps shows it better, mean of 12: the step of b has 0.65 in the changed kernel, 0.87 in r1_rl01 and 1.00 in r5_recip, where its wait is gone, and takes 5.6, 4.4 and 3.9 us. But in r4_early the step of a has no wait for `h` at all and runs at 0.58, since PE stands 2.4 us a slot for `src_a` and then for ACT ahead of it. The Trainium skill (TensorE: Matmul & The Clock Gate, section "HAM oscillation — how this bites in real kernels") says that recurring waits put the array back to its low level each time; the output step of b agrees, with 1.00 against 0.65, and that of a suggests that all waits of the stretch have to go.

**Step a was half right and worth nothing.** The waits of swaps and transposes fell from 4.4 to 2.4. But the turn costs 2.6 instead of 1.7 and the first projection waits 1.4 for `xT` instead of 0.7, so turn, transposes and first projection together stand for 5.8 us before and 5.7 after. What makes the turn longer is open: r3_three gave it back its old first instruction and it stayed at 2.5; in r2_rot and r4_rot, with swaps right ahead of the turn, it is 2.8.

**Step d was right in its place and missed another.** In the last 30 us of a slot, the turn left out, PE stands 2.7 us instead of 4.6, so the spread of PB's projections did help. But the first causal pairs now stand behind the last pairs of the first D group at S+21, and ACT has both and the copies of PA: 1.4 and 0.6 us in the slot shown. The prediction had no term for this.

With the wait for `h` down to 0.95 us (r4_early) a slot takes 156.3 us, not 148. So what R1 said holds for what is left, the waits take other names: with c repaired in three ways the change came out even (0.997 to 0.999), and not 96 us faster. And since the changed kernel has the own tile in it, even means that order, rotation and packs together still cost 0.4 to 1.2% against the tile alone. Whether other places for the same blocks would do better was not shown; no version of the changed kernel was faster beyond its interval.

Aside from this, a sum in the prediction is off: with c, d and e at their better ends the terms give -13.7 a slot and not -12, 2488 and not 2510. It widens the case beyond the range's lower end and has no part in the miss.

The version that beats both kernels is the smallest: the kernel before with the own tile alone, 0.9874 and 0.9929.

## What to carry to other kernels

When a table moves a step, follow its loads through the issuing engine's queue to the tile and the store that each waits for, for every block behind them as well, and cost each from issue to use with the other transfers that go out within the same few us. Count a gain from a removed wait only up to the next wait of the same stretch, and let the clock's share hang on the least certain wait in it. Change one part at a time: here the part costed at nothing was the only one that paid.

## What the runs showed of the hardware

**A load's time from issue to use goes with its neighbours in SP's queue.** Median over 12 slots, where DVE stood waiting for it, from SP's issue of the outputs (two DMAs, 256 KB in all) to the first multiplication:

| neighbours | us |
|---|---|
| six or twelve packs ahead, nothing behind for 3 us (r2_tile, r3_order, before) | 5.5, 5.9, 6.1 |
| x, 512 KB, 1.6 us behind (r2_rot) | 6.6 |
| packs right behind (r4_mult, r4_rot) | 6.8, 7.0 |
| reciprocals issued 1.5 us ahead (r4_early) | 7.8 |
| the same, and packs right behind (b in r1_rl01, a in r4_packs, b in after) | 8.7, 8.8, 9.3 |
| reciprocals 1.5 us behind, which are waited for too, and x (a in after; x moved away, r3_xl) | 9.5; 8.8 |

Twelve packs whose issue ended 0.2 us ahead of it don't delay a load (r2_tile, 5.5). A load issued 1.5 us ahead goes with about 2 us more, packs right behind with about 1 more. Only the last row sets two kernels side by side that differ in one number, so the other differences are read across kernels. The Trainium skill (DMA: Bandwidth & Descriptors, section "Queues, rings and completion order") says that each of the 16 engines takes SP's descriptors in ring order; a delay by a load ahead agrees, with 7.8 against 5.5 to 6.1 us, one by what comes later it would not give.

**DVE is slower beside POOL.** The same subtraction L1353 took 1081 ns in the mean from `xn`, where POOL's additions to x ran beside it, and 677 ns from `on_b`, where they did not:

```profile
L1353 DVE TENSOR_TENSOR h<-xn,h 128x512 fp32r<-128x512 f32 x32 | 33.3, 1081 | 0.0
...
L1353 DVE TENSOR_TENSOR h<-on_b,h 128x512 fp32r<-128x512 f32 x32 | 21.5, 677 | 0.0
```

With three of the four additions left out it was 866 ns. The Trainium skill (SBUF — State Buffer, section "Who interferes with whom") has it that a DVE instruction with two inputs in SBUF contends with a GpSimd instruction that reads SBUF, and the trace agrees.

DVE's busy time rose by 66 us over the program with the same 2972 instructions, 78 us when the instructions are added up one by one, since some overlap. This subtraction is only 12 of the 78. Most is in the layer norms: its scaling (L1395) takes 30 us more, and two steps on tiles of 128x4 take 38. The larger of these, the kernel before first:

```profile
L1386 DVE SCALAR_TENSOR_TENSOR root<-newton,root 128x4 f32<-128x4 f32 x64 | 10.4, 163 | 2.2
...
L1391 DVE SCALAR_TENSOR_TENSOR root<-newton,root 128x4 f32<-128x4 f32 x64 | 37.6, 587 | 1.3
```

Before, none of the 64 had a POOL step beside it. Now 40 have, beside the rotation or the feed-forward, and take 784 and 978 ns in the mean, as long as POOL's step still runs, and the 24 others 154:

```profile
1640.54 1.15 POOL L1565 TENSOR_TENSOR src_b<-tmp,src_b 128x512 f16<-128x512 f32 x1 [0.74 <-ACT src_b L1193]
...
1640.74 0.97 DVE L1391 SCALAR_TENSOR_TENSOR root<-newton,root 128x4 f32<-128x4 f32 x1
```

So a step of 0.16 us can cost DVE 1 us where the table puts it beside POOL. It isn't the change's loss: r1_rl01, even with the kernel before, has the same 978 and 785 ns.
